# Two products of the second attention block, made by GpSimd or by VectorE

## What is computed

```python
q = phi(q)                      # phi(x) = elu(x) + 1
k = phi(k)
kv_cumsum = jnp.cumsum(k * v, axis=2)
k_cumsum = jnp.cumsum(k, axis=2)
out = q * kv_cumsum / (q * k_cumsum + EPS)
```

## Time and profile before

| what | value |
|---|---|
| median of 3 runs | 622.41 us (619.25 to 622.46) |
| the profiled execution | 618.84 us |
| its span, first to last instruction | 617.0 us |
| TensorE matmul busy | 539.3 us (87%), mean granted clock 0.982 |
| VectorE busy | 493.5 us (80%) |
| ScalarE busy | 398.4 us (65%) |
| GpSimd busy | 400.5 us (65%) |
| L566 `den`, 4 on GpSimd | mean 2142 ns |
| L568 `num`, 4 on GpSimd | mean 1283 ns |

### The profile page before, as it was taken

One profiled execution on the slowest core, in us unless ns is written; L12 is line 12 of the kernel. 1 busy time (PEld: TensorE's weight loads), 2 busy tenths in 40 slices (PEclk: granted clock), 3 DMA queues, 4 the chain that ended last, 5 costly groups with the idle time before them and its releaser, 6 DMA issues.

```text
span 617.0 us, 11526 instructions
## 1 busy us (share of the span) xinstructions
PE 539.3 (87%) x4178; PEld 363.9 (59%) x4186; DVE 493.5 (80%) x973; ACT 398.4 (65%) x885; POOL 400.5 (65%) x350
## 2 busy tenths in 40 slices
PE   6569899989899999999987788989999889987992
PEld 2246566656566666666655444545698667654771
DVE  6599999989899888899988989976746966767463
ACT  3497689778777797668887564646776456535230
POOL 1799889899998889888883568822223542434232
PEclk9899999999999999999998999999999998999997
DMA  7155444635454335664344234122010000000001
GB/s 282 35 116 120 108 92 119 101 72 133 74 129 82 69 66 82 170 97 70 68 79 97 93 104 127 44 69 66 16 36 1 1 2 1 1 1 1 1 7 63
DMA packets 98409, 44.64 MB, mean 72 GB/s; under 512 B 88240, under 2 KB 90672, under 8 KB 98352
## 3 DMA queue, kind: packets, MB, share of 16 engines
q1 hardware_dynamic: 97360, 43.35, 30.9%
q10 hardware_dynamic: 992, 0.55, 0.3%
HBM read 21.86 MB, written 1.05 MB: 37 GB/s over the span
## 4 chain that ended last, share of the span: by engine, by line
PE 44%; DVE 24%; POOL 13%; issue 9%; ACT 7%; DMA 2%; SPq 0%; ACTq 0%; POOLq 0%; DVEq 0%
PE bank L1503 39%; PE bank L1670 4%; DVE parts L1105 2%; POOL rr L527 2%; POOL qkl L556 2%; POOL rr L526 2%; DVE w_all_l L1234 2%; POOL qkl L534 2%; DVE nmax L1083 1%; DVE turned L1282 1%; DVE turned L1092 1%; ACT bank L724 1%; DMA bias_v<-in_bvT 1%; DVE vl L1113 1%; DVE ol L1119 1%
## 5 line engine op out<-in xcount | busy, mean ns | idle before, releaser
L1503 PE MATMUL bank<-xTh,w_all_h 128*128 128x512 f16 (+2 forms) x392 | 131.2, 335 | 9.5 <-DVE w_all_l L1039 4.3
L1503 PE MATMUL bank<-xTl,w_all_h 128*128 128x512 f16 (+2 forms) x392 | 131.0, 334 | 0.0
L1503 PE MATMUL bank<-xTh,w_all_l 128*128 128x512 f16 (+2 forms) x392 | 130.8, 334 | 0.0
L556 POOL TENSOR_TENSOR qkl<-turned,qkh 128x512 f16<-128x512 f32 (+1 forms) x44 | 54.0, 1228 | 107.9 <-ACT qkh L838 107.9
L724 ACT ACTIVATE bank<-bank,nmax 128x128 f32<-128x128 f32 (+3 forms) x128 | 64.2, 502 | 46.0 <-DVE nmax L1083 45.7
L526 POOL TENSOR_TENSOR rr<-turned 64x512 f32<-64x512 f32 x64 | 82.3, 1286 | 14.3 <-DVE turned L1094 8.7
L534 POOL TENSOR_TENSOR qkl<-rr,qkh 128x512 f16<-128x512 f32 x64 | 73.8, 1158 | 20.0 <-ACT qkh L743 17.5
L527 POOL TENSOR_TENSOR rr<-turned 64x512 f32<-64x512 f32 x64 | 81.4, 1273 | 3.7
L838 ACT ACTIVATE qkh<-turned 128x512 f16<-128x512 f32 (+1 forms) x44 | 27.6, 628 | 71.7 <-DVE turned L1282 68.0
L1105 DVE SCALAR_TENSOR_TENSOR parts<-bank,rscaled,parts 128x128 f16<-128x128 f32 (+3 forms) x128 | 65.2, 546 | 0.0
L1503 PEld LDWEIGHTS bank<-xTh,w_all_h 128*128 128x128 f16 (+1 forms) x392 | 38.5, 98 | 37.5 <-issue 12.4
(11 more groups left out here) (202 smaller groups left out, 1540.7 us busy)
## 6 DMA issues: line engine op xcount, KB each, us to landing
stage<-in_per_head SPq DMA_DIRECT2D x16, 512.0 KB, 4.0
xa<-in_codes SPq DMA_DIRECT2D x32, 128.0 KB, 2.8
stage<-in_packed SPq DMA_DIRECT2D x12, 256.0 KB, 2.8
stage<-in_scales SPq DMA_DIRECT2D x12, 256.0 KB, 3.3
pT<-parts SPq DMA_TRANSPOSE x128, 2.8
x<-in_x SPq DMA_DIRECT2D x2, 512.0 KB, 7.0
stage<-in_w1T SPq DMA_DIRECT2D x2, 512.0 KB, 4.0
rope<-in_ropes ACTq DMA_DIRECT2D x1, 512.0 KB, 9.5
```

The source lines that it names most:

```text
L556: pool.tensor_tensor(il[n % 2][0:rows, :], inter[0:rows, n % 2, :], ih[n % 2][0:rows, :], ALU.subtract).then_inc(g_il, 1)
L1503: last = pe.matmul(dst, l, r, start=start and i == 0, stop=stop and i == 2, skip_group_check=skip)
```

## The change

`den` and `num` are made by VectorE instead of GpSimd, with the same operation, shapes and operands: 4 units with two multiplies of 128x512 f32. They stand at the head of `inverted(u)`, in front of the epsilon; `weights_of` and its four calls in GpSimd's program go. The semaphores `g_den` and `g_num` go, and with them four waits on VectorE (in `feature` and `running_sums`, for a product that had to be read before its input was written over); `d_num` is new, and `d_den` counts three per unit instead of two.

```diff
--- before.py
+++ after.py
@@ -241,8 +241,7 @@
         d_carry = sem("d_carry")
         d_cum = sem("d_cum")
         d_ksum = sem("d_ksum")
-        g_den = sem("g_den")
-        g_num = sem("g_num")
+        d_num = sem("d_num")
         d_den = sem("d_den")
         d_att = sem("d_att")
         a_atth = sem("a_atth")
@@ -556,17 +555,6 @@
                 pool.tensor_tensor(il[n % 2][0:rows, :], inter[0:rows, n % 2, :], ih[n % 2][0:rows, :],
                                    ALU.subtract).then_inc(g_il, 1)
 
-            def weights_of(u):
-
-                rows = phi[u % 2][:, 1, :]
-                pool.wait_ge(d_ksum, u + 1)
-                pool.wait_ge(d_phi, 2 * u + 2)
-                if u:
-                    pool.wait_ge(d_att, u)
-                pool.tensor_tensor(den, rows, k_sum, ALU.mult).then_inc(g_den, 1)
-                pool.wait_ge(d_cum, u + 1)
-                pool.tensor_tensor(num, rows, kv_sum, ALU.mult).then_inc(g_num, 1)
-
             def rstd_of(phase, part, what):
 
                 n, rows = event(phase, part, what), row_slice(part)
@@ -606,11 +594,8 @@
                     rstd_of(1, 0, "y")
                 if m == 1:
                     rstd_of(1, 0, "x")
-                if m == 5:
-                    weights_of(0)
                 if m == 7:
                     low_att(0)
-                    weights_of(1)
                 if m == 8:
                     rstd_of(1, 2, "y")
                     low_att(1)
@@ -620,8 +605,6 @@
                     rstd_of(2, 0, "y")
                 if m == 11:
                     rstd_of(2, 0, "x")
-                if m == 14:
-                    weights_of(2)
             for m in range(I_TILES):
                 if m == 0:
                     low_att(2)
@@ -633,7 +616,6 @@
                     rstd_of(2, 2, "y")
                 if m == 2:
                     rstd_of(2, 2, "x")
-                    weights_of(3)
                 if m == 5:
                     low_att(3)
             for m in range(I_TILES):
@@ -1286,8 +1268,6 @@
             def feature(u, w):
 
                 dve.wait_ge(a_expo, 2 * u + w + 1)
-                if u >= 2:
-                    dve.wait_ge(g_num, u - 1)
                 dve.scalar_tensor_tensor(out=phi[u % 2][:, w, :], in0=expo[:, w, :], scalar=1.0, in1=pos[:, w, :],
                                          op0=ALU.min, op1=ALU.add).then_inc(d_phi, 1)
 
@@ -1308,23 +1288,25 @@
                     dve.wait_ge(d_cum, u)
                     dve.tensor_tensor(kv[:, firsts], kv[:, firsts], kv_sum[:, lasts], ALU.add).then_inc(d_carry, 1)
                     dve.wait_ge(d_carry, u + 1)
-                if u:
-                    dve.wait_ge(g_den, u)
                 dve.tensor_tensor_scan(k_sum, ones, keys, 0.0, ALU.mult, ALU.add).then_inc(d_ksum, 1)
-                if u:
-                    dve.wait_ge(g_num, u)
                 dve.tensor_tensor_scan(kv_sum, ones, kv, 0.0, ALU.mult, ALU.add).then_inc(d_cum, 1)
 
             def inverted(u):
 
-                dve.wait_ge(g_den, u + 1)
+                rows = phi[u % 2][:, 1, :]
+                dve.wait_ge(d_ksum, u + 1)
+                dve.wait_ge(d_phi, 2 * u + 2)
+                dve.tensor_tensor(den, rows, k_sum, ALU.mult).then_inc(d_den, 1)
+                dve.wait_ge(d_cum, u + 1)
+                dve.tensor_tensor(num, rows, kv_sum, ALU.mult).then_inc(d_num, 1)
+                dve.wait_ge(d_den, 3 * u + 1)
                 dve.tensor_scalar(den, den, CUM_EPS, None, ALU.add).then_inc(d_den, 1)
-                dve.wait_ge(d_den, 2 * u + 1)
+                dve.wait_ge(d_den, 3 * u + 2)
                 dve.reciprocal(den, den).then_inc(d_den, 1)
 
             def attend(u):
-                dve.wait_ge(d_den, 2 * u + 2)
-                dve.wait_ge(g_num, u + 1)
+                dve.wait_ge(d_den, 3 * u + 3)
+                dve.wait_ge(d_num, u + 1)
                 if u:
                     dve.wait_ge(g_attl, u)
                 dve.tensor_tensor(att, num, den, ALU.mult).then_inc(d_att, 1)
```

## The result

| | median | lowest to highest | runs |
|---|---|---|---|
| before | 620.69 us | 618.12 to 623.21 | 20 |
| changed | 623.83 us | 620.97 to 627.84 | 20 |

The ratio is 1.0055, with a 95% interval of 1.0037 to 1.0074: 3.4 us slower (2.3 to 4.6 us of 620.69), the difference of the medians is 3.1. The kernel is slower, just past the 0.5% that a measurement can tell, where I had put it just inside.

What follows compares the result with a forecast made beforehand. VectorE was taken to bound the second attention, ending or just preceding TensorE's waits except GpSimd's at 566.76. Units 0 to 3 add 1.22 + 1.48 + 0 + 0.2 = +2.9 to 622.41, giving 625.3 us, range 621.2 to 628.3.

Steps and rivals of the forecast that it cites:

- VectorE is on the path from the reciprocal on, TensorE waits for `weighted(1)`: Second attention: from unit 1's reciprocal added VectorE time costs its full length; TensorE waits 0.30 us at 481.52 for `weighted(1)`.
- Unit 0, +1.22: Second attention's unit 0: two VectorE multiplies delay the epsilon through `weighted(1)` and TensorE's `look_up(6)`, without cover, by 1.22 us.
- Unit 1, +1.48: Unit 1: multiplies 1.22, plus 0.84 with den held by GpSimd's low half of tile 8, minus 0.58 from a faster epsilon.
- Unit 2, 0: Unit 2: `attend(2)` 0.6 to 0.9 us late, covered by VectorE's 2.08 us idle before 540.88; up to +0.9 without cover.
- Unit 3, +0.2: Unit 3: 0.93 us gained at tile 3's low half ends in a VectorE-set wait; 1.46 later minus 1.25 cover gives 0.21.
- 1.17 us idle: Unit 3: VectorE's idle time before tile 5's product at 572.68, counted as cover against the epsilon ending 1.46 us later.
- The sum, +2.9: Whole kernel: 1.22 + 1.48 + 0 + 0.2 = +2.9 us, 0.47% slower; forecast chance 0.50.
- 625.3 us, from 622.41: Forecast time: 622.41 us, the median of the runs shown, plus 2.9 gives 625.3.
- The clock in the new gap: TensorE's granted clock falls in run 2 behind the wait at 481.52, grown to 1.52 us: +4.4, 626.8 us; chance 0.18.
- VectorE keeps its turn in unit 3: Unit 3: the epsilon goes ahead of GpSimd's low half, -0.7 us there; total +2.0, 624.4 us; chance 0.17.
- GpSimd was the bound: Waits at 481.52 and 510.52 have slack, so only unit 3's 0.93 us gain counts: -0.9, 621.5 us; chance 0.05.
- Nothing to see: Delays of units 0 and 1 are made up before 540 by TensorE's waits: 0 to +1, 622.9 us; chance 0.10.

Runs made afterwards that it cites:

- units 0, 1 and 3 alone: Three kernels, each the one before with only that unit's two multiplies on VectorE; only unit 3's was timed: 620.63 us, ratio 1.0010.
- the early multiplies: Changed kernel with only unit 0's two multiplies moved ahead of feature(1, 0), into VectorE's idle 3.08 us; no time given.
- units 0 and 1: Kernel before with the multiplies of units 0 and 1 on VectorE, 2 and 3 on GpSimd; 622.13 us against 620.37, ratio 1.0028.
- GpSimd kept off: Changed kernel where GpSimd waits for unit 1's num before taking the low half of tile 8; den 0.66 us instead of 1.40, no time given.

## Why the prediction was right, and where not

- **VectorE is on the path from the reciprocal on, TensorE waits for `weighted(1)`.** Right. The 0.30 us wait was enough to say that unit 0 had no slack.
- **Unit 0, +1.22.** Right: 1.22 in the changed kernel, 1.21 alone, and 1.20 back when only the place changes.
- **Unit 1, +1.48.** The mechanism was right and the holding a little smaller: 0.72 instead of 0.84, so 1.32 to 1.33. VectorE got in before GpSimd's row had ended (`den` ends at 491.85, 0.55 behind 491.30, where it takes 0.68 alone). Keeping GpSimd away took off 0.74. The rule of the Trainium skill that the later one blocks for the whole of the other (page "SBUF — State Buffer", section "SBUF: two separate sides") agrees with that in kind; taken to the letter it gave 0.84, and the runs show 0.72 to 0.74.
- **Unit 2, 0.** Right: 0.62 later and covered.
- **Unit 3, +0.2.** The forecast of what happens was right (0.87 gained at the low half where 0.93 was expected, the epsilon beside tile 4's low half, and the reciprocal 1.29 later where 1.46 was expected), and the size right for the execution that I had: 0.04. It is wrong as a forecast of a median. The step that failed is the subtraction of "1.17 us idle" before tile 5's product. That idle time was TensorE at half clock, in an execution that happened to have it. Where the clock stays up there is no idle time, and the term is +1.29, beyond the +0.8 that I gave as its upper end. The prediction itself names "the half clock behind it" at 566.76, in the rival on GpSimd, and did not see that the 1.17 us came from it; so the 0.04 of that execution is no merit of the +0.2.
- **The sum, +2.9.** With the clock halved in unit 3: 2.54 + 0.04 = 2.6. Without: 2.54 + 1.29 = 3.8. Measured 3.4 (2.3 to 4.6) by the ratio and 3.1 by the medians, between the two. Of the eight profiled kernels with GpSimd's products in unit 3, two had the fall, which is few to go by; weighted so, an estimate of the term is 0.75 x 1.29 + 0.25 x 0.04 = 1.0, and of the sum 3.5. That +2.9 is so near to it is in part luck: unit 1 was 0.16 too large and unit 3 by this estimate 0.8 too small. The forecast of 0.47% and the measured 0.55% lie on either side of the 0.5% line, where I had given 0.53 and 0.42; the interval (0.37 to 0.74%) reaches over both sides. The 0.05 that I gave to "faster" was for a rival of -0.9 us, which is 0.14% and by the same line no change.
- **625.3 us, from 622.41.** The median of before over 20 runs is 620.69; the three runs shown stood 1.7 us high. The change was 0.5 too small (0.2 by the medians) and the base 1.7 too large, which has nothing to do with the change; the changed kernel came at 623.83, inside 621.2 to 628.3.
- **The rivals.** The clock in the new gap: not seen, 1.00 from 483 to 496 in the profiled execution. VectorE keeps its turn in unit 3: no, the last part took 22.77 or 22.78 in all six executions with that unit on VectorE. GpSimd was the bound: in unit 3 its wait did shrink, by 0.87, and the gain was gone at the next wait. Nothing to see: no, the second distance is 2.54 longer.

## What to carry to other kernels

An operation moved to the engine that is faster at it costs what that engine's order makes of it: 1.22 us in front of a wait that others stand behind, and nothing in an idle gap one instruction earlier. Idle time in one profiled execution is cover only if its cause is steady; look whether the engine waited for was at its full clock. And in a kernel with a spread of 5 us between runs, distances between two instructions of one engine tell fractions of a microsecond that no median will.

## What the runs showed of the hardware

- TensorE's clock behind the same gap falls in some executions and not in others. Behind the wait of 2.81 us the way to the wait for `low_half(2, 3)` takes 42.00 to 42.02 us in five of the fourteen profiled executions (units 0, 1 and 3 alone, the early multiplies, units 0 and 1) and 43.20 to 43.48 in the others, before and changed among them. Behind the wait in unit 3 it was half in four (before, changed, units 0 and 1, GpSimd kept off) and full in ten, at waits of 3.1 us as at waits of 2.2. A fall behind the wait of 2.81 costs 1.2 to 1.5 us of the way behind it. One in unit 3 costs 1.24 us of the last part with the products on GpSimd (22.73 and 22.75 against 21.49 and 21.50) and nothing with them on VectorE (22.77 and 22.78 either way). What makes it fall or not is open; that the change alters how often was not shown (mean clock over the span 0.976 in 20 runs of the changed kernel, 0.977 in 29 of before).
- A VectorE multiply with two SBUF inputs and a GpSimd operation hold each other off: unit 1's `den` takes 1.40 beside GpSimd's low half and 0.66 without, and the low half of tile 4 in unit 3 takes 1.51, as it starts beside VectorE's `num`, where that of tile 3 takes 1.15. Very small GpSimd operations are held too (the sum of 1/std 0.67 instead of 0.23), but hold nobody measurably (`num` beside it takes 0.68).
